# Self-attention on one core: the tile's probabilities are turned before the scores of two tiles ahead, instead of after

## The chip, the cores and the metric

The kernel runs on one NeuronCore of a Trainium2 chip. A NeuronCore has engines with instruction streams of their own, which meet only through semaphores: TensorE (PE in the profile; PEld is its weight loads), VectorE (DVE), ScalarE (ACT), GpSimd (POOL) and SyncE (SP, which issues DMAs). The metric is the time on the device of one execution in microseconds; the median over several runs is quoted.

## What is computed

The kernel is a chain of four transformer parts on an input of 2 x 512 tokens of width 128. Two of them hold a self-attention with 16 heads of width 64; these two are what the change touches. Cut to what matters:

```python
# first part, per batch of 512 tokens, h = adaptive layernorm of x
q, k, v = h @ wq, h @ wk, h @ wv                 # 16 heads of 64
attn = softmax(q @ k.T / sqrt(64))               # 512 x 512 per head
x = (attn @ v) @ wo + bo + x
...
# second part: the same sizes, with biases, a rotary turn of q and k, and a causal mask
q, k = rope(q + q_b), rope(k + k_b)
attn = softmax(where(causal, q @ k.T / sqrt(64), -inf))
```

After them come a cross-attention and a gated feed-forward in the first part, 32 experts in the second, six transformer layers with 8-wide heads in the third and 64 experts in the fourth. None of their code is changed.

## The kernel before

Both self-attentions are one function, `self_attention_block`, called with the name A1 (tiles `A_...` in the profile) and with the name B1 (`B_...`). It works through 16 pairs of heads (8 pairs, two batches). A pair n has four tiles t of 128 queries; step i = 4n + t is one tile of the two heads. In A1 a tile has 512 keys, in B1 it has 128 (t + 1), for the causal mask. Five pieces belong to a tile:

- `scores(i)` (TensorE, L631): two matmuls, one for each head, into two of four PSUM banks, alternating between even and odd tiles; in B1 two small matmuls (L635) add the mask. It waits until the exponentials of tile i - 2 have left its banks, and at t = 0 until q and k of the pair are there.
- `row_max(i)` (VectorE, L817): the negated maximum of each row, of both heads at once.
- `exps(i)` (ScalarE, L729): two exponentials with their row sums, from PSUM to `prob`.
- `weights(i)` (VectorE, L823 and L826): the reciprocal of the sums, and two multiplications of `prob` in place.
- `turn(i)` (TensorE, L647): the 2 x keys/128 transposes of the normalised tile into banks of a ring of three (4, 5, 7); ScalarE's `copy_turned(i)` (L739) empties them into `probT`.

Pair by pair there are also the projections of q, k and v of pair n + 2 (L615, L612), the product with v of pair n - 1 (`weigh`, L661) and the output projection of pair n - 2 (`project_out`, L669). VectorE takes q and k out of PSUM (`take`; L796 and L798 in A1). In B1 ScalarE adds the bias (L717), VectorE multiplies by the cosine (L805), and a DMA and GpSimd do the sine half of the rotary turn (L567, L570).

Each engine's order is written out by hand, as a loop over i, and each engine runs its own list in that order. TensorE's list in a step before the change: `scores(i + 2)`, `turn(i)`, `weigh(n - 1, t)`, one projection of pair n + 2 at t below 3, and `project_out(n - 2)` at t = 3. VectorE's: an output addition (L834) at t = 0, `take` at t = 1 and 2, `row_max(i + 2)`, `weights(i + 1)`, and then small pieces of norms or of the router that were put there to fill. ScalarE's: the copy of a context at t = 0, in B1 a raw copy at t = 1 and 2, `copy_turned(i)`, the copy of v at t = 2, `exps(i + 2)`.

Of the kernel before, what the change touches and what calls it, by code (L numbers as in the profile page):

```python
# [493 lines left out]
def self_attention_block(nc, m, name, w, w_loaded, rope=None, bias=None, tail=None, opening=None):  # L494
# [28 lines left out]
    def turned(i):  # L523

        n, t = divmod(i, TB)
        if 2 * keys(t) <= S:
            return [(("p", i, 0), (0, 1))]
        return [(("p", i, 0), (0,)), (("p", i, 1), (1,))]
# [12 lines left out]
    with nc.sbuf_tensor(name + "_q", [P, 3, S], F32) as qT, \  # L541
# [43 lines left out]
        def _(pe):  # L585
# [4 lines left out]
            def fill(key):  # L590
                bank = RING[len(turns) % len(RING)]
                turns.append(key)
                uses[bank] += 1
                place[key] = bank, uses[bank]
                if uses[bank] > 1:
                    pe.wait_ge(emptied[bank], uses[bank] - 1)
                return bank
# [3 lines left out]
            def project(n, what):  # L601
                if n not in begun:
                    begun.append(n)
                    for (first, _), loaded in zip(W_PARTS, w_loaded):
                        if first == n:
                            pe.wait_ge(loaded, 16)
                    if n == PAIRS and opening is not None:
                        drained(pe, "turn_norm")
                bank = fill((what, n))
                if what == "v":  # L610
                    for t in range(TB):
                        last = pe.matmul(ps[:, bank, t * P:(t + 1) * P], lhsT=hT(n)[:, t * P:(t + 1) * P],  # L612
                                         rhs=weight(n, WV), start=True, stop=True)
                else:
                    last = pe.matmul(ps[:, bank, :], lhsT=weight(n, column[what]), rhs=hT(n), start=True, stop=True)  # L615
                last.then_inc(filled[bank], 1)

            def scores(i):
                n, t = divmod(i, TB)
                if t == 0:  # L620
                    if rope is None:
                        drained(pe, ("q", n))
                        drained(pe, ("k", n))
                    else:
                        pe.wait_ge(q_ready, n + 1)
                        pe.wait_ge(k_ready, n + 1)
                if i >= 2:
                    pe.wait_ge(exp_done, 2 * (i - 1))
                first = S_BANK + 2 * (i % 2)
                for h in range(2):  # L630
                    last = pe.matmul(ps[:, first + h, 0:keys(t)], lhsT=qT[half(h), n % 3, t * P:(t + 1) * P],  # L631
                                     rhs=kT[half(h), n % 3, 0:keys(t)], start=True, stop=not causal)
                if causal:
                    for h in range(2):
                        last = pe.matmul(ps[:, first + h, t * P:(t + 1) * P], lhsT=m.identb[:], rhs=m.maskq[:],  # L635
                                         start=False, stop=True)
                last.then_inc(s_done, 1)

            def turn(i):
                n, t = divmod(i, TB)  # L640
                pe.wait_ge(p_ready, 2 * (i + 1))
                for key, heads in turned(i):
                    bank = fill(key)
                    for j, h in enumerate(heads):
                        for kt in range(keys(t) // P):
                            col = j * keys(t) + kt * P
                            last = pe.transpose(ps[:, bank, col:col + P], prob[:, i % 2, h, kt * P:(kt + 1) * P],  # L647
                                                m.ident[:])
                    last.then_inc(filled[bank], 1)

            def weigh(n, kt):
                if kt == 0:
                    drained(pe, ("v", n))
                    for t in (TB - 2, TB - 1):
                        for key, _ in turned(n * TB + t):
                            drained(pe, key)
                    if n:
                        pe.wait_ge(cT_ready, n)
                q0 = first_q(kt)
                for h in range(2):  # L660
                    last = pe.matmul(ps[half(h), PV_BANK, q0:S], lhsT=v[:, n % 4, kt, half(h)],  # L661
                                     rhs=probT[:, n % 2, kt, h, q0:S], start=kt == 0, stop=kt == TB - 1)
                last.then_inc(pv_done, 1)

            def project_out(n):
                pe.wait_ge(cT_ready, n + 1)
                bank = fill(("out", n))
                for t in range(TB):
                    last = pe.matmul(ps[:, bank, t * P:(t + 1) * P], lhsT=cT[:, n % 2, t * P:(t + 1) * P],  # L669
                                     rhs=weight(n, WO), start=True, stop=True)  # L670
                last.then_inc(filled[bank], 1)
# [9 lines left out]
                project(1, what)  # L681
            for i in range(STEPS):
                n, t = divmod(i, TB)
                if i + 2 < STEPS:
                    scores(i + 2)
                turn(i)
                if n:
                    weigh(n - 1, t)
                if n + 2 < N and t < 3:
                    project(n + 2, "qkv"[t])  # L690
                if t == TB - 1 and n >= 2:
                    project_out(n - 2)
                if opening is not None and (n, t) == (PAIRS - 4, 3):
                    bank = fill("turn_norm")
                    opening.outer[1].turn(pe, ps[:, bank, :]).then_inc(filled[bank], 1)
                if tail is not None:
                    tail.tensor(pe, n, t, ring)
# [2376 lines left out]
```

## Time and profile before

| | |
|---|---|
| time, median of 3 runs | 2410.42 us (2408.8 to 2411.71) |
| the profiled execution | 2412.81 us, of which 2411.0 us are the span of the trace |
| TensorE matmuls | 2076.3 us busy (86%), 10944 instructions |
| VectorE | 1533.4 us (64%) |
| ScalarE | 1267.0 us (53%) |
| GpSimd | 233.7 us (10%) |
| granted TensorE clock, mean | 0.931 of full speed |

The profiled execution lies 2.4 us above the median. The shares are averages over parts with different limits; the two self-attentions lie at about 23 to 290 us and 450 to 682 us of the span. A busy TensorE in this table means that matmuls follow each other, with ends that the profiler models.

### The profile page before, as it was taken

What the parts mean: (1) busy time and instruction counts of PE and PEld (TensorE: products, weight loads), DVE (VectorE), ACT (ScalarE), POOL (GpSimd) and SP (SyncE); (2) the same over time, 40 slices, a digit from 0 to 9 for tenths busy, and PEclk for the clock granted to TensorE, in tenths of its full rate; (3) what the DMA queues carried; (4) which work ended last, traced back from release to release, by engine and by line L of the source; (5) the groups of instructions that cost most, each with busy time, mean ns of one, the idle gap of its engine ahead of it and who ended that gap; (6) DMA issues with size and microseconds to landing.
All of it is one profiled execution on the core that took longest, in us unless ns stands there. A gap on an engine that the chain in (4) does not pass through costs nothing.

```text
span 2411.0 us, 32117 instructions
## 1 busy us (share of the span) xinstructions
PE 2076.3 (86%) x10944; PEld 913.2 (38%) x10944; DVE 1533.4 (64%) x3684; ACT 1267.0 (53%) x2430; POOL 233.7 (10%) x235
## 2 busy tenths in 40 slices
PE   7999998799999888788878887887888788868998
PEld 3444465455566422322233223323222322233433
DVE  6867576666757777467656755774667467553564
ACT  4666553477643356546636563656466556625311
POOL 0000000243320200100010001100010101020000
PEclk9999999799999989979988997999799979979999
DMA  4000000411010110001000100100110001020000
GB/s 157 1 1 1 1 1 1 137 41 40 32 56 3 47 27 1 13 15 46 1 27 1 46 1 27 40 7 1 27 46 1 25 3 28 27 84 1 1 0 9
DMA packets 43154, 61.66 MB, mean 26 GB/s; under 512 B 6097, under 2 KB 35570, under 8 KB 41586
## 3 DMA queue, kind: packets, MB, share of 16 engines
q1 hardware_dynamic: 42994, 59.61, 7.7%
q8 instruction: 90, 1.47, 0.2%
q14 instruction: 70, 0.57, 0.1%
HBM read 31.28 MB, written 0.52 MB: 13 GB/s over the span
## 4 chain that ended last, share of the span: by engine, by line
PE 42%; DVE 10%; ACT 9%; issue 4%; SPq 0%; POOL 0%; ACTq 0%; DMA 0%; DVEq 0%
PE ps L1969 8%; PE ps L1949 5%; ACT big L2457 4%; PE ps L1930 4%; DVE C_nm L2634 4%; PE ps L2014 3%; PE ps L2097 3%; PE ps L2204 2%; PE ps L2200 2%; PE ps L2225 2%; PE ps L2109 2%; ACT big L2537 2%; PE ps L2116 2%; PE ps L2125 2%; PE ps L2074 2%
## 5 line engine op out<-in xcount | busy, mean ns | idle before, releaser
L2634 DVE TENSOR_REDUCE C_nm<-ps 128x1 f32<-128x512 f32 x768 | 500.2, 684 | 214.3 <-PE ps L1930 211.7
L2457 ACT ACTIVATE big<-ps 128x512 f32<-128x512 f32 x768 | 427.7, 596 | 230.6 <-PE ps L1949 220.6
L1930 PE MATMUL ps<-C_attn 62*128 62x512 bf16 x768 | 277.5, 420 | 58.7 <-DVE C_nm L2634 51.1
L1949 PE MATMUL ps<-C_attn 64*128 64x512 bf16 x768 | 253.0, 396 | 64.6 <-ACT big L2457 55.4
L1969 PE MATMUL ps<-big,C_attn 128*32 128x512 f32 x1536 | 214.3, 631 | 14.4 <-ACT big L2457 14.4
L1930 PEld LDWEIGHTS ps<-C_attn 62*128 62x128 bf16 x768 | 63.3, 94 | 296.1 <-DVE C_nm L2634 157.2
L1949 PEld LDWEIGHTS ps<-C_attn 64*128 64x128 bf16 x768 | 59.2, 93 | 279.9 <-ACT big L2457 206.3
L2537 ACT ACTIVATE big<-ps,C_biasx 77x512 f32<-77x512 f32 x192 | 115.5, 678 | 56.4 <-PE ps L2101 56.3
L2390 POOL TENSOR_SCALAR lnv<-mv 128x4 f32<-128x4 f32 x36 | 8.2, 227 | 1218.0 <-DVE mv L2616 1218.0
L2596 ACT ACTIVATE big<-ps 128x512 f32<-128x512 f32 (+1 forms) x66 | 39.4, 597 | 150.0 <-PE ps L2200 149.9
L817 DVE TENSOR_REDUCE A_nm<-ps 128x2 f32<-128x1024 f32 x64 | 78.3, 1224 | 42.6 <-PE ps L631 42.2
L2949 DVE TENSOR_TENSOR big<-big,ps 128x512 f32<-128x512 f32 x64 | 44.0, 687 | 94.5 <-PE ps L2204 74.3
L2724 DVE TENSOR_REDUCE C_nmx<-ps 128x4 f32<-128x308 f32 x192 | 78.0, 471 | 40.5 <-PE ps L2078 40.2
L739 ACT ACTIVATE A_pT<-ps 128x512 f32<-128x512 f32 x128 | 69.6, 598 | 63.6 <-PE ps L647 63.6
L2014 PE MATMUL ps<-C_hT,C_w 128*128 128x512 f32 x144 | 86.1, 705 | 10.7 <-ACT C_hT L2481 5.3
L2841 DVE SCALAR_TENSOR_TENSOR y<-ps,cn,y 128x128 f32<-128x128 f32 x256 | 72.0, 344 | 33.8 <-PE ps L2043 32.8
L729 ACT ACTIVATE A_p<-ps,A_nm 128x512 f32<-128x512 f32 x128 | 87.3, 699 | 9.4 <-DVE A_nm L817 9.4
L2564 ACT ACTIVATE pair<-ps,big 128x512 f32<-128x512 f32 x64 | 43.9, 687 | 78.0 <-PE ps L2036 77.9
L2043 PEld LDWEIGHTS ps<-big,pair 128*128 128x128 f32 x512 | 67.3, 193 | 35.7 <-issue 31.3
L2656 DVE RECIPROCAL C_rden<-ps 128x16 f32<-128x16 f32 x96 | 24.3, 253 | 88.7 <-PE ps L1977 53.3
L729 ACT ACTIVATE B_p<-ps,B_nm 128x128 f32<-128x128 f32 (+3 forms) x128 | 66.3, 526 | 20.9 <-DVE B_nm L817 20.8
L2097 PE MATMUL ps<-C_qx,C_kc 32*77 32x512 f32 x384 | 66.3, 764 | 12.4 <-issue 6.6
(369 smaller groups left out, 3769.1 us busy)
## 6 DMA issues: line engine op xcount, KB each, us to landing
C_attn<-C_first SPq DMA_DIRECT2D x144, 128.0 KB, 2.4
B_rot<-B_rot SPq DMA_DIRECT2D x64, 128.0 KB, 2.0
C_w<-in_C_w SPq DMA_DIRECT2D x6, 1090.0 KB, 5.3
C_attn<-in_D_ew SPq DMA_DIRECT2D x4, 1536.0 KB, 10.2
big<-in_B_ew SPq DMA_DIRECT2D x8, 514.0 KB, 9.1
normw_later<-in_norm_w SPq DMA_DIRECT2D x1, 2304.0 KB, 16.1
A_w<-in_A_w SPq DMA_DIRECT2D x2, 1024.0 KB, 11.2
A_w<-in_A_w SPq DMA_DIRECT2D x2, 768.0 KB, 11.7
```

Of the source, the lines that this page charges most:

```text
L729: act.activation(prob[:, i % 2, h, 0:keys(t)], ps[:, S_BANK + 2 * (i % 2) + h, 0:keys(t)], ACT.Exp, bias=nm[:, i % 2, h:h + 1], accum_out= ...
L817: dve.tensor_reduce(nm[:, i % 2, :], ps[:, first:first + 2, 0:keys(t)], AX.X, ALU.max, negate=True)\
L1930: pe.matmul(ps[:, bank, :], lhsT=qs[side(hp, MAX_ROW), b, 2 * q + pq, t * P:(t + 1) * P], rhs=ks[side(hp, MAX_ROW), b, 2 * q + pq, :], sta ...
L1949: pe.matmul(ps[:, bank, :], lhsT=ks[side(1 - hp, HALF), b, 2 * q + pq, kt * P:(kt + 1) * P], rhs=qs[side(1 - hp, HALF), b, 2 * q + pq, :], ...
L1969: last = pe.matmul(ps[ct * VW:(ct + 1) * VW, PV_BANK, :], lhsT=va[:, b, kt, q * QUAD + ct, :], rhs=prob[:, kt % 2, ct // 2, ct % 2, :], st ...
L2014: pe.matmul(ps[:, bank, :], lhsT=weight(n, col), rhs=hT[:], start=True, stop=True)\
L2097: pe.matmul(ps[0:CTX, banks[r], :], lhsT=cross.k[rows, c, q, :], rhs=qx[rows, :], start=True, stop=False)
L2457: act.activation(prob[:, kt % 2, pq, 1 - hp, :], ps[:, bank, :], ACT.Exp, scale=SCALE)\
L2537: act.activation(probx[:, q % 2, r, :], ps[0:CTX, bank, :], ACT.Exp, bias=cross.bias[:, b:b + 1], scale=SCALE).then_inc(emptied[bank], 1)
L2634: dve.tensor_reduce(nm[:, q % 2, t, pq, hp:hp + 1], ps[:, bank, :], AX.X, ALU.max, negate=True).then_inc(emptied[bank], 1)
L2724: dve.tensor_reduce(nmx[:, t, 4 * r:4 * r + 4], ps[:, bank, 0:4 * CTX].rearrange("p (j k) -> p j k", k=CTX), AX.X, ALU.max, negate=True).t ...
L2841: dve.scalar_tensor_tensor(y, ps[:, bank, t * P:(t + 1) * P], e_b.gates[:, b * TB + t, e:e + 1], y, ALU.mult, ALU.add).then_inc(y_added if ...
```

## The change

Two statements of TensorE's loop change places. In a step TensorE now issues `turn(i)` first and `scores(i + 2)` second; all other engines' lists, the buffers, the waits and the semaphore counts are the same. `scores` uses no bank of the ring, so the banks that the ring hands out are the same too.

```diff
@@ -681,9 +681,9 @@
                 project(1, what)
             for i in range(STEPS):
                 n, t = divmod(i, TB)
+                turn(i)
                 if i + 2 < STEPS:
                     scores(i + 2)
-                turn(i)
                 if n:
                     weigh(n - 1, t)
                 if n + 2 < N and t < 3:
```

## Rows read from the trace of the kernel before

**Rows 1.** Busy time by stretch: inside A1, all of B1, a stretch of B1.

```profile
core 0: us, PE busy (x) PEld busy (x) DVE busy (x) ACT busy (x) POOL busy (x), PEclk, DMA share, GB/s
109.07:258.30 149.23, 149.23 (x758) 71.62 (x756) 106.02 (x206) 96.35 (x235) 0.00 (x0) 1.00 0.00 1
460.00:674.00 214.00, 201.95 (x1214) 107.24 (x1213) 154.35 (x342) 148.53 (x401) 83.00 (x60) 0.98 0.10 38
601.90:612.00 10.10, 8.48 (x53) 5.94 (x54) 8.72 (x23) 5.64 (x17) 4.63 (x4) 0.83 0.08 28
```

**Rows 2.** Timeline, one step of A1: start, duration, engine, line, operation.

```profile
153.79 1.13 PE L631 MATMUL ps<-A_k,A_q 64*128 64x512 f32 x4
...
154.97 1.23 DVE L817 TENSOR_REDUCE A_nm<-ps 128x2 f32<-128x1024 f32 x1 [1.97 <-PE ps L631]
...
156.30 0.88 DVE L826 TENSOR_SCALAR A_p<-A_p,A_inv 128x512 f32<-128x512 f32 x2
...
157.97 1.13 PE L631 MATMUL ps<-A_k,A_q 64*128 64x512 f32 x4
```

**Rows 3.** Timeline, the first steps of A1, TensorE.

```profile
30.80 1.13 PE L631 MATMUL ps<-A_k,A_q 64*128 64x512 f32 x4
...
40.72 1.09 PE L647 MATMUL ps<-ident,A_p 128*128 128x128 f32 x8
...
41.75 1.13 PE L631 MATMUL ps<-A_k,A_q 64*128 64x512 f32 x4
```

**Rows 4.** Timeline, near the end of A1: the multiplications and the turn of tile 62.

```profile
277.38 0.88 DVE L826 TENSOR_SCALAR A_p<-A_p,A_inv 128x512 f32<-128x512 f32 x2
...
278.31 1.09 PE L647 MATMUL ps<-ident,A_p 128*128 128x128 f32 x8 [0.28 <-DVE A_p L826]
```

**Rows 5.** Timeline, one pair of B1, four steps.

```profile
541.59 0.92 PE L631 MATMUL ps<-B_k,B_q 64*128 64x384 f32 x4
...
542.76 0.96 DVE L817 TENSOR_REDUCE B_nm<-ps 128x2 f32<-128x768 f32 x1 [0.38 <-PE ps L635]
...
544.94 1.13 PE L631 MATMUL ps<-B_k,B_q 64*128 64x512 f32 x4
...
546.42 1.22 DVE L817 TENSOR_REDUCE B_nm<-ps 128x2 f32<-128x1024 f32 x1
...
547.75 0.75 DVE L826 TENSOR_SCALAR B_p<-B_p,B_inv 128x384 f32<-128x384 f32 x2
...
548.51 0.49 PE L631 MATMUL ps<-B_k,B_q 64*128 64x128 f32 x4
...
549.77 0.69 DVE L805 TENSOR_TENSOR B_k<-B_rot,B_cos 128x512 f32<-128x512 f32 x1 [1.28 <-ACTq L720]
...
550.38 0.42 DVE L817 TENSOR_REDUCE B_nm<-ps 128x2 f32<-128x256 f32 x1
...
550.91 1.36 DVE L826 TENSOR_SCALAR B_p<-B_p,B_inv 128x512 f32<-128x512 f32 x2
...
551.48 0.70 PE L631 MATMUL ps<-B_k,B_q 64*128 64x256 f32 x4
...
552.44 0.69 DVE L817 TENSOR_REDUCE B_nm<-ps 128x2 f32<-128x512 f32 x1 [0.17 <-PE ps L635]
...
553.24 0.68 DVE L826 TENSOR_SCALAR B_p<-B_p,B_inv 128x128 f32<-128x128 f32 x2
...
554.81 0.92 PE L631 MATMUL ps<-B_k,B_q 64*128 64x384 f32 x4
```

**Rows 6.** Timeline, VectorE and GpSimd in a later pair of B1.

```profile
602.70 1.27 POOL L570 TENSOR_TENSOR B_q<-B_q,B_rot 128x512 f32<-128x512 f32 x1
...
602.71 1.81 DVE L805 TENSOR_TENSOR B_k<-B_rot,B_cos 128x512 f32<-128x512 f32 x1
```

**Rows 7.** Timeline, TensorE: turn of the first tile of B1's pair 1.

```profile
476.81 0.39 PE L647 MATMUL ps<-ident,B_p 128*128 128x128 f32 x2
```

**Rows 8.** Timeline, TensorE: turns of B1's tiles 56 and 62.

```profile
655.26 0.39 PE L647 MATMUL ps<-ident,B_p 128*128 128x128 f32 x2
...
670.98 0.87 PE L647 MATMUL ps<-ident,B_p 128*128 128x128 f32 x6 [0.39 <-DVE B_p L826]
```

## The prediction

> **What bounds the kernel now.** I read the page first, then the busy time by stretch, then the timelines of single steps. The page says that TensorE is busy most of the span, but what counts is the two self-attentions. By stretch, TensorE is busy for all of 149.23 us of 149.23 inside A1, and for 201.95 of 214.00 us in B1, at a granted clock of 1.00 and 0.98 [rows 1]. So both are bound by TensorE's own work; VectorE is busy 71% and 72% there. The reader should see in the timeline that in A1 one step follows the next after 4.18 us (scores at 153.79 and at 157.97) with four pieces of TensorE work in it, and that VectorE, after its row maximum, has to wait 1.97 us for the next scores [rows 2]. In B1 a pair takes 13.22 us, from the scores at 541.59 to those at 554.81, by the same rule [rows 5]. A change of TensorE's order adds and removes no work. It can gain only idle TensorE time, of which A1 has none and B1 12 us, and it loses if it makes a chain through the other engines longer than TensorE's own work.
>
> **The chain that the change closes.** No instruction is added; what moves is the eight or fewer transposes of turn(i), with their weight loads, past the scores of tile i + 2. No DMA moves. The new wait is in the order: scores(i + 2) now stands behind turn(i), which waits for weights(i). Now look at VectorE, whose list is row_max(i + 2), then weights(i + 1). The row maximum waits for scores(i + 2); weights(i + 1), whose exponentials were ready long before, is queued behind it; and turn(i + 1) on TensorE waits for weights(i + 1). So turn(i), scores(i + 2), row_max(i + 2), weights(i + 1), turn(i + 1) become one chain, and a step cannot be shorter than that. Before, the scores came ahead of the turn, and the chain from one turn to a later one spread over two steps: the multiplications ended at 157.18 (156.30 + 0.88) [rows 2], some 1.9 us ahead of the turn that needs them, which follows the scores of 157.97.
>
> **A1, one step.** Turn to scores, when the one follows the other directly: 40.72 to 41.75, 1.03 us [rows 3]. Start of scores to start of the row maximum: 153.79 to 154.97, 1.18 us; start of the row maximum to the end of the multiplications: 154.97 to 157.18, 2.21 us [rows 2]. End of the multiplications to the turn that waits for them: 278.26 to 278.31, 0.05 us [rows 4]. Sum: 4.47 us, against TensorE's 4.18 us in a full step and about three quarters of that in the steps of the first and last pairs that have only three pieces. The chain wins in all of them. What VectorE does besides (taking q or k, 512 columns like the 0.69 us product of [rows 5], and small pieces of norms) falls into the 2.26 us in which it now waits for turn and scores; ScalarE's copies fall into its idle time, 53 us of 149 [rows 1]. I cost both at nothing; without that cover each would add its excess over 2.26 us, once.
>
> The first turn can start at 30.80, where the scores of tile 2 stand now [rows 3]; 62 steps of 4.47 us bring the turn of tile 62 to 307.9, where it is at 278.31 now [rows 4]: +29.6 us. Two steps carry four more transposes of a norm (4 x 0.13 us), so TensorE's 4.7 us sets them: +0.4. A1: **+30 us**. Bounds: 4.42 us a step if the 0.05 us is already in the rows, 4.57 if TensorE restarts 0.1 us later after a wait: +27 to +36.
>
> **B1, one pair.** The four steps differ, because tile t has 128 (t + 1) keys. Scores to row maximum is 1.17 us for 384 keys and 0.96 us for 256 [rows 5]; by the difference I take 1.38 for 512 and 0.75 for 128. A transpose is 0.13 us. From the turn at t = 0 as zero:
> - t = 0: the chain (two transposes, 384 keys) is shorter than TensorE's work, 541.59 to 544.94 [rows 5]. Turn of t = 1 at 3.35.
> - t = 1: 0.52 for four transposes and 1.38 bring the row maximum of 512 keys to 5.25. The multiplications would end 2.08 us later (546.42 to 548.50 [rows 5]): turn of t = 2 at 7.38.
> - t = 2: the row maximum of 128 keys stands behind VectorE's cosine product, which waits for a raw copy on ScalarE, which is queued behind the exponentials of the 512 keys. That path from row maximum to row maximum is 546.42 to 550.38, 3.96 us [rows 5]; so 9.21, later than the scores allow. The multiplications end 1.89 us on (550.38 to 552.27): turn of t = 3 at 11.15.
> - t = 3: 1.03 for eight transposes, 0.96, then 552.44 to 553.92 [rows 5], 1.48, and 0.05: next pair at 14.67.
>
> That is 14.67 us against 13.22. VectorE and GpSimd also get in each other's way here. A cosine product that took 0.69 us [rows 5] took 1.81 us where a GpSimd addition had started 0.01 us before it [rows 6], so a new phase can cost up to 1.12 us a pair: 15.8 at most. If on the contrary the raw copy held nothing up and the multiplications of 512 keys took A1's 0.88 us [rows 2] and not 1.36 [rows 5], it would be 13.9. I take 14.9, a fifth of the way up, because the delayed product leaves the multiplications behind it undelayed.
>
> The Trainium skill, "SBUF — State Buffer", section "SBUF: two separate sides", says that VectorE's products of two SBUF operands and GpSimd share a port pair as an exclusive lock, and that the one that comes second is blocked for the other's whole instruction. Rows 6 agree: 1.81 us where the other took 1.27. By that rule alone, with GpSimd first in every pair, the pair would be 15.8 us and the total 12 us above mine.
>
> Pairs 1 to 13 take 178.45 us now, from 476.81 [rows 7] to 655.26 [rows 8], 6.6 us over 13 x 13.22, through the router's pieces. Half of that should hide in VectorE's new waits (an estimate): 13 x 14.9 + 3.3 = 197.0, +18.6. The last six steps with scores take 15.72 us now (655.26 to 670.98 [rows 8]); without projections and GpSimd the chain gives about 3.1, 4.0, 3.0, 3.5, 3.1 and 4.0, 20.7, +5.0. Pair 0 has no product with v and gains up to 3 us of chain: +1.5. B1: **+25 us**. Bounds +7 (13.9 us a pair, all pieces hidden, nothing for pair 0) and +42 (15.8, nothing hidden, 3 us for pair 0).
>
> **Sum.** +30 and +25 are +55 us. The profiled execution, 2412.8 us with 1.8 us around its span, would become 2468; on the median of 2410.4 that is **2466 us**. Nothing after either block starts early enough to take it back: both end in a barrier.
>
> **Rivals.**
> 1. The clock falls. In 601.90 to 612.00 TensorE was idle 1.62 us, and the granted clock was 0.83, between the levels of 1.2 and 2.4 GHz [rows 1]: 10.10 x 0.17, 1.7 us of work lost. The change makes idle gaps of 1 to 1.5 us in each pair of B1 and in some nine steps of A1. A fall in each of these 22 places is +37 us: 2503. Against it: 0.3 us of idleness in a 4.47 us step leaves A1 94% busy, the share that B1 has now at 0.98.
> The skill's "TensorE: Matmul & The Clock Gate", Part 1, says that the throttled clock is the default and sustained activity releases it; rows 1 agree in the direction, and by it this rival only adds to the loss.
> 2. Only A1 pays, because B1's pairs stay near 13.9 us and its pieces hide: +30 and a few, about 2443.
> 3. TensorE stays the bound and nothing changes: 2410. That needs a chain under 4.18 us, 0.29 us less than the rows give, as if VectorE took weights(i + 1) before row_max(i + 2). Its list says otherwise.
> 4. It gets faster: with that same chain hidden, a turn that is ready would no longer wait behind scores that wait for q and k out of the rotary turn, as in B1's first pair. It decides only from a chain under 4.18 us on, and its ceiling is B1's idle 12 us [rows 1]: 2398.
>
> **Chances and range.** The forecast holds 0.76, the falling clock 0.10, A1 alone 0.06, no change 0.04, faster 0.04. The bounds of both blocks give +34 to +78, 2444 to 2488; rivals 2 and the mild form of 1 lie at its ends. About 0.2%, 5 us, is what a measurement here can tell from no change: slower 0.92, within it 0.04, faster 0.04.
>
> **What would show it.** In A1, scores 4.47 us apart in every step, with TensorE idle about 0.3 us before the turn, released by VectorE's L826, and some 1.4 us in the steps without projection; the first multiplications' end followed by a turn within 0.1 us. VectorE's row maximum waits for L631, and weights follows at once. A1 ends 30 us later at a clock of 1.00. In B1 pairs of 14.7 to 15.2 us, with the longest step at t = 2. After both, everything at its old length. The prediction is wrong if turns do not wait for L826, if A1's steps stay at 4.18, or if the clock falls below 0.95 in either block.

## The result, and the profile after

| | before | after |
|---|---|---|
| time, median | 2409.61 us (2406.32 to 2411.71, 4 runs) | 2489.8 us (2484.65 to 2496.45, 4 runs) |
| span of the profiled execution | 2411.0 us | 2490.6 us |
| TensorE matmuls busy | 2076.3 us | 2093.2 us |
| mean granted clock | 0.931 | 0.929 |

The ratio is 1.0336, with an interval of 1.0306 to 1.0365: 80 us slower. The forecast was 2466 us, with 2444 to 2488 as its range, so the time came out 24 us above the forecast and 2 us above the range. The 79.6 us by which the span grew lie like this, read from the first and last turns of the two blocks: A1 ends 29.0 us later (its last turn starts at 309.38 instead of 280.35), the stretch between the blocks gives back 1.0, B1 is 52.2 us longer, and the rest gives back 0.6. A1 did what was forecast; B1 did twice as much.

**A1.** The timeline of one step of the kernel after, which answers to [rows 2]. Columns: start, duration, engine, line, operation, and in brackets the idle time before it and what ended it.

```profile
150.61 1.09 PE L647 MATMUL ps<-ident,A_p 128*128 128x128 f32 x8 [0.22 <-DVE A_p L826]
...
151.63 1.13 PE L631 MATMUL ps<-A_k,A_q 64*128 64x512 f32 x4
...
152.81 1.22 DVE L817 TENSOR_REDUCE A_nm<-ps 128x2 f32<-128x1024 f32 x1 [2.25 <-PE ps L631]
...
154.14 0.88 DVE L826 TENSOR_SCALAR A_p<-A_p,A_inv 128x512 f32<-128x512 f32 x2
...
155.08 1.09 PE L647 MATMUL ps<-ident,A_p 128*128 128x128 f32 x8 [0.22 <-DVE A_p L826]
```

The reader should walk the chain link by link: turn at 150.61, scores 1.02 us later, the row maximum 1.18 after those, the end of the multiplications at 155.02, and the next turn 0.06 after that, 4.47 us in all. Each row either waits for the one above it or stands behind it in its engine's list. The waits from 29 to 290 us, grouped by who waited for whom (us in total, times, longest), say the same for most steps; in the kernel before, the second of these rows read 0.5 us for two waits.

```profile
DVE A_nm L817 <- PE ps L631: 85.1, 58, 2.3
...
PE ps L647 <- DVE A_p L826: 22.0, 56, 2.3
```

**B1.** Busy time by stretch, kernel after: B1's pair 0, pairs 1 to 13 and pairs 14 and 15, and at last all of A1 (columns as in [rows 1]: length, busy time of PE, PEld, DVE, ACT and POOL, PEclk, DMA share).

```profile
488.74:510.54 21.80, 14.56 (x58) 8.27 (x56) 13.53 (x20) 9.80 (x26) 10.66 (x8) 0.68 0.13 48
510.54:729.91 219.37, 188.64 (x1045) 99.50 (x1045) 138.37 (x274) 125.36 (x339) 69.22 (x52) 0.94 0.09 32
729.91:753.59 23.68, 17.98 (x111) 8.55 (x109) 15.55 (x48) 13.53 (x39) 0.00 (x0) 1.00 0.00 1
29.51:309.38 279.87, 253.68 (x1269) 119.47 (x1269) 180.85 (x378) 170.13 (x404) 0.00 (x0) 1.00 0.00 1
```

The same three stretches of the kernel before:

```profile
460.76:476.81 16.05, 10.70 (x59) 6.07 (x57) 14.74 (x19) 8.32 (x23) 10.77 (x8) 0.89 0.18 66
476.81:655.26 178.45, 173.81 (x1046) 92.40 (x1045) 124.16 (x275) 127.21 (x344) 72.23 (x52) 0.99 0.11 39
655.26:673.40 18.14, 16.08 (x104) 7.95 (x103) 14.77 (x47) 12.35 (x36) 0.00 (x0) 1.00 0.01 2
```

Pair 0 pays 5.75 us (forecast 1.5), pairs 1 to 13 pay 40.9 (forecast 18.6), the last two 5.5 (forecast 5.0 for their six steps). VectorE's busy time in the middle row is 14.2 us longer although its instructions are the same: something stretches them. One pair of B1 shows what, in the timeline of the kernel after, which answers to [rows 5, 6]:

```profile
535.82 0.87 PE L647 MATMUL ps<-ident,B_p 128*128 128x128 f32 x6 [0.32 <-DVE B_p L826]
...
536.97 1.27 POOL L570 TENSOR_TENSOR B_q<-B_q,B_rot 128x512 f32<-128x512 f32 x1
...
537.04 1.75 DVE L805 TENSOR_TENSOR B_k<-B_rot,B_cos 128x512 f32<-128x512 f32 x1 [1.28 <-ACTq L720]
...
538.71 0.41 DVE L817 TENSOR_REDUCE B_nm<-ps 128x2 f32<-128x256 f32 x1
...
540.17 1.09 PE L647 MATMUL ps<-ident,B_p 128*128 128x128 f32 x8 [1.17 <-DVE B_p L826]
...
542.95 1.49 DVE L826 TENSOR_SCALAR B_p<-B_p,B_inv 128x128 f32<-128x128 f32 x2
543.03 1.32 POOL L570 TENSOR_TENSOR B_k<-B_k,B_rot 128x512 f32<-128x512 f32 x1
...
544.49 0.44 PE L647 MATMUL ps<-ident,B_p 128*128 128x128 f32 x2 [0.93 <-DVE B_p L826]
```

GpSimd's addition for q starts 0.07 us ahead of VectorE's cosine product for k, and the product takes 1.75 us instead of 0.69; then GpSimd's addition for k starts 0.08 us behind the multiplications of the next tile, and these take 1.49 instead of 0.48, which is their time one pair earlier (at 527.83). The 0.68 of [rows 5] is not their undisturbed time: there too a GpSimd product was running, from 552.38 to 553.65. Both stand in the closed chain, and TensorE's turn waits for both. Grouped by line, the cosine product of k reads so before, and then after (count, busy time, mean ns):

```profile
L805 DVE TENSOR_TENSOR B_k<-B_rot,B_cos 128x512 f32<-128x512 f32 x16 | 14.2, 889 | 15.5 <-ACTq L720 15.3
```

```profile
L805 DVE TENSOR_TENSOR B_k<-B_rot,B_cos 128x512 f32<-128x512 f32 x16 | 23.4, 1462 | 14.4 <-ACTq L720 14.2
```

Of its 16 instances 12 took 1.4 us or more, against 3 before. The Trainium skill, "SBUF — State Buffer", section "SBUF: two separate sides", describes VectorE and GpSimd excluding each other on a shared pair of ports; the trace agrees, with 1.75 us for 0.69.

**The clock in B1.** The timeline of TensorE in pair 0 of the kernel after, and below it the busy time of pair 1, pairs 2 to 8 and pairs 9 to 13 (columns as above):

```profile
493.25 1.12 PE L647 MATMUL ps<-ident,B_p 128*128 128x128 f32 x4 [2.15 <-DVE B_p L826]
494.30 2.08 PE L631 MATMUL ps<-B_k,B_q 64*128 64x512 f32 x4
...
500.25 1.54 PE L647 MATMUL ps<-ident,B_p 128*128 128x128 f32 x6 [2.66 <-DVE B_p L826]
```

```profile
510.54:528.36 17.82, 15.44 (x72) 6.99 (x72) 9.45 (x18) 9.09 (x26) 5.13 (x4) 0.82 0.08 31
528.36:639.41 111.05, 95.69 (x561) 50.17 (x561) 69.84 (x133) 68.17 (x185) 37.57 (x28) 1.00 0.09 34
639.41:729.91 90.50, 77.51 (x413) 42.35 (x413) 59.09 (x124) 48.10 (x129) 26.53 (x20) 0.89 0.08 30
```

After 2.15 us of idleness the scores of 512 keys, 1.13 us elsewhere, take 2.08; the granted clock reads 0.50 from 493.2 to 496.4, the lower of TensorE's two levels, 1.2 GHz. The granted clock is 0.68 over pair 0 and 0.94 over pairs 1 to 13, against 0.89 and 0.99 before. Pairs 2 to 8 run at 1.00 and are slow all the same, 15.86 us each. In A1 the clock stays at 1.00.

### The profile page after: what moved, and what is told of

It is laid out like the page before. It is cut to its first block, busy times and chain, and to the rows that moved or that the text cites. A ratio compares the mean times of both kernels' runs of the same rounds, so it can differ in the third digit from the quotient of the medians.

```text
span 2490.6 us, 32117 instructions
## 1 busy us (share of the span) xinstructions
PE 2093.2 (84%) x10944; PEld 921.9 (37%) x10944; DVE 1543.8 (62%) x3684; ACT 1271.5 (51%) x2430; POOL 230.8 (9%) x235
## 4 chain that ended last, share of the span: by engine, by line
PE 39%; DVE 10%; ACT 8%; issue 4%; SPq 1%; DMA 0%; POOL 0%; ACTq 0%; DVEq 0%
PE ps L1969 7%; PE ps L1949 5%; ACT big L2457 4%; PE ps L1930 4%; DVE C_nm L2634 4%; PE ps L2097 3%; PE ps L2014 2%; PE ps L2204 2%; PE ps L2200 2%; PE ps L2225 2%; ACT big L2537 2%; PE ps L2109 2%; PE ps L2116 2%; PE ps L2125 2%; PE ps L2074 1%
## 5 line engine op out<-in xcount | busy, mean ns | idle before, releaser
L817 DVE TENSOR_REDUCE B_nm<-ps 128x2 f32<-128x256 f32 (+1 forms) x64 | 52.6, 822 | 68.9 <-PE ps L635 68.5
L647 PE MATMUL ps<-ident,A_p 128*128 128x128 f32 x512 | 70.2, 280 | 26.8 <-DVE A_p L826 26.2
L647 PE MATMUL ps<-ident,B_p 128*128 128x128 f32 x320 | 52.5, 299 | 40.6 <-DVE B_p L826 39.1
## 6 DMA issues: line engine op xcount, KB each, us to landing
normw_later<-in_norm_w SPq DMA_DIRECT2D x1, 2304.0 KB, 15.8
```

The source lines that it names most:

```text
L817: dve.tensor_reduce(nm[:, i % 2, :], ps[:, first:first + 2, 0:keys(t)], AX.X, ALU.max, negate=True)\
```

## The experiments

The theory was that turn, scores, row maximum and multiplications form one chain, closed by VectorE's list; that the chain alone sets A1; and that in B1 collisions with GpSimd stretch it. The rival was that the turn's place itself, or the clock, costs the time. The ratios below are to the kernel before, run beside each.

**Opening the chain.** The changed kernel, with VectorE's list turned round in both blocks:

```diff
+                if i + 1 < STEPS:
+                    weights(i + 1)
                 if i + 2 < STEPS:
                     row_max(i + 2)
-                if i + 1 < STEPS:
-                    weights(i + 1)
```

> The changed kernel with VectorE's list turned as well: weights(i + 1) ahead of row_max(i + 2). Theory (the chain is closed by VectorE's order): turn(i + 1) no longer waits for scores(i + 2), the chain is spread over two steps again and TensorE's own work sets the step. A1: steps of 4.15 to 4.18 us, B1: pairs of 13.2 to 13.8 us, time within 12 us of the kernel before, 2398 to 2422. Rival (it is turn(i)'s own wait for weights(i) that holds the scores up, whatever VectorE's order is): A1 stays at 4.47 us a step and the time above 2465.

2439.41 us (2433.78 to 2440.79), ratio 1.0093 (1.0066 to 1.0119): 23 us over the kernel before. That lies between the two expectations: A1's steps came out shorter than the theory's 4.15 to 4.18 us, B1's pairs longer than its 13.2 to 13.8. By block, A1 takes 254.8 us from first to last turn (changed kernel 279.9, before 248.5) and B1 236.4 (264.9 and 212.6). The timeline of A1 in this kernel:

```profile
145.09 1.08 PE L661 MATMUL ps<-A_pT,A_v 128*64 128x512 f32 x4 [0.38 <-ACT A_cT L748]
...
151.06 1.04 PE L647 MATMUL ps<-ident,A_p 128*128 128x128 f32 x8
...
152.16 0.88 DVE L826 TENSOR_SCALAR A_p<-A_p,A_inv 128x512 f32<-128x512 f32 x2
...
155.09 1.04 PE L647 MATMUL ps<-ident,A_p 128*128 128x128 f32 x8
```

The multiplications end at 153.04, 2.05 us before the turn that needs them, and the step from 151.06 to 155.09 is 4.03 us: the chain is open, and in these steps the new place of the turn costs nothing by itself. What is left in A1 is one step in four, at t = 0, of 4.44 to 4.51 us in most pairs, where the product with v now waits for ScalarE's copy of the context (first row), and the three-piece steps. In B1's pairs 2 to 8 a pair takes 14.5 to 15.3 us, and the step at t = 2 still 4.28 to 4.97.

**What still holds B1.** The same kernel, with VectorE's `take` moved behind the multiplications too, so that its list is `weights(i + 1)`, `take`, `row_max(i + 2)`:

```diff
+                if i + 1 < STEPS:
+                    weights(i + 1)
                 if n + 2 < N and t in (1, 2):
                     take(n + 2, t - 1)
                 if i + 2 < STEPS:
                     row_max(i + 2)
-                if i + 1 < STEPS:
-                    weights(i + 1)
```

> Theory: in B1 what still held the turn after VectorE took the multiplications ahead of the row maximum was the cosine product that stood ahead of both and waits for ScalarE's raw copy. With the product behind the multiplications the longest step of a pair (t = 2, 4.35 to 4.97 us) falls to about 3.7, a pair of B1 from 14.8 to 13.3 to 13.7 us, B1 from 236 to 215 to 222, and the total lies 5 to 16 us above the kernel before (A1's 6 us stay). Rival: the product stands in front of the row maximum in any case, so the wait only moves there, a pair stays over 14.3 us and the total 20 us or more above.

2437.87 us (2433.23 to 2442.12), ratio 1.011 (1.0088 to 1.0132). In B1 the theory held in the main: the step at t = 2 is 3.24 us in most of pairs 2 to 8, a pair there about 13.8 (13.3 to 13.7 expected), and the block 224.15 us (215 to 222 expected), 12 less than in the experiment above. The total missed the theory's 5 to 16 us and stayed 25 above the kernel before, where the rival had it, though not by the rival's pairs of over 14.3 us. A1 took back half of the gain, 6 us; the other half is no more than the intervals of the two runs leave open. A1's first and last turn now lie 260.7 us apart, with steps of 4.22 to 4.36 us at t = 2, where the projection of v waits for the later `take` of k:

```profile
158.58 0.97 PEld L612 LDWEIGHTS ps<-A_w,hT 128*128 128x128 f32 x8 [1.01 <-DVE A_k L798]
```

In B1 of the same timeline a collision stretches the multiplications to 1.90 us and costs the turn only 0.30, since they start early:

```profile
533.74 1.90 DVE L826 TENSOR_SCALAR B_p<-B_p,B_inv 128x512 f32<-128x512 f32 x2
...
533.85 1.50 POOL L570 TENSOR_TENSOR B_q<-B_q,B_rot 128x512 f32<-128x512 f32 x1
...
535.69 0.86 PEld L647 LDWEIGHTS ps<-ident,B_p 128*128 128x128 f32 x8 [0.30 <-DVE B_p L826]
```

**One block at a time.** The new order under `if rope is None` (A1 alone) and under `if rope is not None` (B1 alone), as an edit of the kernel before:

```diff
+                if rope is None:          # the other kernel: is not None
+                    turn(i)
                 if i + 2 < STEPS:
                     scores(i + 2)
-                turn(i)
+                if rope is not None:      # the other kernel: is None
+                    turn(i)
```

> The new order in A1 alone, B1 in the old order. Theory (62 steps of 4.47 us, nothing given back): +29 us, 2439. Rival (the profiled spans of A1 overstate it, part is hidden at the barrier or in later loads): +20 or less. B1's first turn to last turn stays at 213 us in both.

> The new order in B1 alone, A1 in the old order. Theory (both blocks add, B1's loss is of its own making): +51 us, 2461, with the same three lengths of step as in the changed kernel, 3.4, 4.05 and 4.35 or 5.43 us. Rival (B1's extra loss comes from a phase or a clock that A1's longer run left behind): +25 to +35, 2435 to 2445.

A1 alone: 2448.47 us, ratio 1.0131 (1.0097 to 1.0165), +32. B1 alone: 2467.83, ratio 1.0215 (1.0189 to 1.0241), +52. Together 84, against 80 for the whole change, which is equal within the intervals: the blocks don't touch each other, and the shares read from the trace (29 and 52) are right.

**GpSimd taken out of the way.** In the changed kernel and in the kernel before, GpSimd's product and addition (L567, L570) work on 8 of 512 columns, so most of the sine half of the rotary turn is left out; all waits stay.

```diff
-    pool.tensor_tensor(turned_rows, turned_rows, rope[i][1], ALU.mult).then_inc(sin_done, 1)
+    pool.tensor_tensor(turned_rows[:, 0:8], turned_rows[:, 0:8], rope[i][1][:, 0:8], ALU.mult)\
+        .then_inc(sin_done, 1)
...
-    pool.tensor_tensor(dst[:, n % 3, :], dst[:, n % 3, :], turned_rows, ALU.add)\
+    pool.tensor_tensor(dst[:, n % 3, 0:8], dst[:, n % 3, 0:8], turned_rows[:, 0:8], ALU.add)\
```

> The changed kernel with GpSimd's sine product and addition cut to 8 of 512 columns, so that most of the rotary turn's sine half is left out; all waits and the order stay. Theory (what my sum missed in B1 is VectorE's multiplications and cosine products blocked behind GpSimd's): pairs 2 to 8 fall from 15.9 to about 14.2 us (the chain's 14.67 less the 0.48 us that the multiplications of 512 keys lose), t = 2 and t = 3 have one length each, and the time falls by 20 to 35 us to 2455 to 2470. Rival 1 (the raw copy on ScalarE and the order alone): pairs stay at 15.4 to 15.9 and the time above 2480. Rival 2 (the clock): the pairs at a lower clock, 0, 1 and 9 to 13, keep their length.

> The kernel before with the same cut as the run before it (GpSimd's sine product and addition on 8 of 512 columns, most of the sine half left out). Theory (GpSimd blocks VectorE off TensorE's path in the old order, except in the first pair and the router's pairs): pairs 2 to 8 stay at 13.2 us, only the first pair and pairs 10 to 13 gain; 6 to 14 us faster, 2402 to 2410. Rival (GpSimd's work costs the old order as much as the new, so the cut says nothing of the change): 40 us or more faster.

Changed kernel with the cut: 2447.78 us, ratio 1.0145 (1.011 to 1.0179). Against the changed kernel's 1.0336 that is 1.9% of the kernel before, some 46 us, and more than expected. Kernel before with the cut: 2396.53, ratio 0.9928 (0.9902 to 0.9954), 17 us faster, a little more than the 6 to 14 expected. Busy time by stretch, the same three stretches of B1, first the changed kernel with the cut, then the kernel before with it:

```profile
487.81:502.19 14.38, 9.61 (x57) 5.16 (x57) 8.91 (x20) 9.72 (x26) 1.72 (x8) 1.00 0.20 75
502.19:689.26 187.07, 178.78 (x1045) 94.90 (x1045) 111.35 (x274) 123.24 (x339) 12.73 (x52) 0.99 0.10 37
689.26:712.94 23.68, 17.98 (x110) 8.55 (x109) 15.56 (x48) 13.53 (x39) 0.00 (x0) 1.00 0.01 1
```

```profile
452.67:465.13 12.46, 10.66 (x58) 6.60 (x57) 8.17 (x20) 8.46 (x23) 1.73 (x8) 0.86 0.23 85
465.13:637.52 172.39, 170.49 (x1047) 90.72 (x1045) 110.77 (x275) 126.98 (x344) 10.70 (x52) 1.00 0.11 41
637.52:655.67 18.15, 16.08 (x104) 7.95 (x103) 14.78 (x47) 12.36 (x36) 0.00 (x0) 1.00 0.01 2
```

Without GpSimd's work the change costs B1 1.9 + 14.7 + 5.5 = 22.1 us, and with it 52.2. So 30 of B1's 52 us come from VectorE and GpSimd meeting. Less work on GpSimd also makes q and k ready earlier, but that is not where the time goes: from 488 to 754 us of the changed kernel no wait of TensorE, VectorE or ScalarE is put down to GpSimd. The clock came back in the same run, from 0.68 and 0.94 to 1.00 and 0.99; the two gaps of pair 0 are then 1.30 and 1.26 us instead of 2.15 and 2.66, so in the changed kernel the falls go with the waits that the collisions made. (The kernel before stays at 0.86 in its pair 0 even so.) In pairs 2 to 8 the changed kernel's clock is 1.00 with GpSimd's work and without it, and a pair takes 15.86 and 14.07 us: 12.6 us over these seven pairs are stretched instructions alone, against 0.9 in the same pairs of the kernel before. How the rest divides between the stretched instructions and the lower clock behind them was not measured.

**A known delay put into the chain.** A memset of 128 x 512 on VectorE between `row_max` and `weights`, in A1 alone, in the kernel before and in the changed kernel:

```diff
                 if i + 2 < STEPS:
                     row_max(i + 2)
+                if rope is None:
+                    c.after(dve.memset(pad[:], 0.0))
                 if i + 1 < STEPS:
                     weights(i + 1)
```

> The kernel before with a memory set of 128 x 512 put into VectorE's list between row_max(i + 2) and weights(i + 1), in A1 alone; it costs VectorE an estimated 0.5 us a step. Theory (the multiplications end some 1.9 us before the turn needs them): hidden in every full step, 4.15 to 4.18 us a step as before; 0 to +4 us from the steps with three pieces. Rival (VectorE's time counts in the old order too): +25 to +35 us.

> The changed kernel with the same memory set at the same place, in A1 alone. Theory (row_max and weights lie on the closed chain, so every addition between them counts in full): A1's steps grow from 4.47 us by the whole cost of the memory set, about 5.0 us, and the time by 62 times that, +25 to +37 us over the changed kernel, 2515 to 2527. Rival (TensorE's pieces or ScalarE's set the 4.47 us): under +8.

Before: 2412.26 us, ratio 0.9997 (0.9977 to 1.0017); nearly all full steps stay at 4.15 to 4.18 us, and A1 is 2.7 us longer, as expected. Changed: 2546.81, ratio 1.0551 (1.0522 to 1.0579), 2.15% or 52 us over the changed kernel, of which 46 lie in A1 (325.6 us from first to last turn). That is more than expected, since the size was off: the delay with the wait for its completion is 0.66 us, not the memset's 0.48. The timeline of the changed kernel with the memset (lines below it are moved by one):

```profile
150.18 1.09 PE L648 MATMUL ps<-ident,A_p 128*128 128x128 f32 x8 [0.89 <-DVE A_p L827]
...
152.45 1.23 DVE L818 TENSOR_REDUCE A_nm<-ps 128x2 f32<-128x1024 f32 x1 [1.26 <-PE ps L632]
...
153.73 0.48 DVE L856 MEMSET A_pad<- 128x512 f32 x1
154.25 0.17 DVE L824 RECIPROCAL A_inv<-A_sums 128x2 f32<-128x2 f32 x1
...
155.38 1.09 PE L648 MATMUL ps<-ident,A_p 128*128 128x128 f32 x8 [0.95 <-DVE A_p L827]
```

From the row maximum's start to the reciprocal it is 1.80 us instead of 1.14, and nearly all full steps take 5.14 instead of 4.47: the delay comes out whole. The kernel before hides the same delay whole. That is the difference between a chain that sets the step and one with slack.

**The order that pays.** From the kernel before, in A1's pairs 1 to 13 alone: the turn first and the multiplications first; and, in all of A1, ScalarE's copy of the context moved from t = 0 to t = 3 of the pair before, ahead of the exponentials. Everything else keeps its order.

```diff
+                if rope is None and 1 <= n <= N - 3:
+                    turn(i)
                 if i + 2 < STEPS:
                     scores(i + 2)
-                turn(i)
+                if not (rope is None and 1 <= n <= N - 3):
+                    turn(i)
...
+                early = rope is None and 1 <= n <= N - 3
+                if early:
+                    weights(i + 1)
                 if i + 2 < STEPS:
                     row_max(i + 2)
-                if i + 1 < STEPS:
+                if i + 1 < STEPS and not early:
                     weights(i + 1)
...
-                if t == 0 and n >= 2:
+                if t == 0 and n >= 2 and rope is not None:
                     copy_context(n - 2)
...
+                if rope is None and t == 3 and 1 <= n < N - 1:
+                    copy_context(n - 1)
```

> The new order with VectorE's weights(i + 1) first, in the full steps of A1 alone (pairs 1 to 13), and the copy of the context on ScalarE moved from the head of a pair to the step before, ahead of its exponentials; B1 and A1's other pairs in the old order. Theory (with the chain open, TensorE's pieces follow each other in 4.00 to 4.03 us where the old order took 4.15 to 4.18, and the first step of a pair loses 0.45 us only to that copy): pairs of 16.1 us instead of 16.65, 5 to 8 us faster than the kernel before, ratio 0.997. Rival (the shorter steps are paid back at the borders of the pairs): within 0.2% of before.

2405.87 us (2398.05 to 2416.0, 12 runs) against 2413.4 for the kernel before on that chip; ratio 0.9976 (0.9957 to 0.9996). It is 0.24% faster than the kernel before, an interval that only just excludes no change, and the fastest of those tried that leave nothing out. The timeline of TensorE:

```profile
163.49 1.04 PE L647 MATMUL ps<-ident,A_p 128*128 128x128 f32 x8
...
164.45 1.13 PE L631 MATMUL ps<-A_k,A_q 64*128 64x512 f32 x4
...
165.51 1.08 PE L661 MATMUL ps<-A_pT,A_v 128*64 128x512 f32 x4
...
166.52 1.16 PE L612 MATMUL ps<-A_w,hT 128*128 128x128 f32 x8
167.52 1.04 PE L647 MATMUL ps<-ident,A_p 128*128 128x128 f32 x8
```

No row waits, and the step is 4.03 us. The block takes 242.9 us instead of 248.5.

**The same for B1.** The last kernel, with B1's pairs 1 to 13 in the new order too, and there VectorE's list `weights`, `take`, `row_max`.

> The faster version of A1, and in B1's pairs 1 to 13 the turn first with VectorE's list multiplications, cosine product, row maximum. By the theory a pair of B1 takes 13.0 to 13.7 us against 13.1 to 13.3 before, so the total is within 8 us of the version that changes A1 alone, on either side. By the rival a pair stays over 14.3 us and the total is 12 us or more above the kernel before.

2414.95 us, ratio 1.0014 (1.0001 to 1.0027), 9 us over the version that changes A1 alone and so a little outside the 8 us expected; the two were run on different chips. B1's pairs 2 to 8 take 13.6 to 14.7 us, 13.9 on average, just above the theory's 13.0 to 13.7, and the block 222.6 us against 212.6. The chain is open in B1 as well, but collisions still reach the turn (steps of 3.9 to 4.2 us where 3.2 is usual), and the new order gains nothing there.

## Why the prediction was right in A1 and short in B1

- **TensorE bounds both blocks, and a change of order can only lose or gain idle time.** Right: the instructions are the same and no new kind of work appeared.
- **The chain.** Right, and shown from both sides: the turn waits for L826 in 56 steps of A1; taking the multiplications ahead of the row maximum brings the step from 4.47 to 4.03 us; a delay of 0.66 us in the chain lengthens the step by 0.67.
- **A1: 4.47 us a step, +30 us.** Measured 4.45 to 4.47 us in 51 of the 62 steps (4.52 to 4.62 in the others), and the block ends 29.0 us later, at a clock of 1.00.
- **B1, the steps at t = 0 and t = 1.** 3.40 and 4.05 us against 3.35 and 4.03. Right.
- **B1, the steps at t = 2 and t = 3.** This is the step that failed: "a new phase can cost up to 1.12 us a pair: 15.8 at most". I allowed one collision a pair, priced it at a fifth, and called its full price the bound. The price of one collision was right (1.75 against 0.69 us is 1.06), but it came in 12 of 16 pairs, and in five of pairs 2 to 8 a second one came, at t = 2 or at t = 3. A pair took 15.86 us on average in pairs 2 to 8 (528.36 to 639.41) and 18.1 in pairs 9 to 13 (639.41 to 729.91). The wrong thought behind it was "the delayed product leaves the multiplications behind it undelayed": GpSimd does one product and one addition for q and one of each for k, and in a chain without slack each of the four can meet something. A second collision, from the timeline of the kernel after:

```profile
570.50 1.97 DVE L826 TENSOR_SCALAR B_p<-B_p,B_inv 128x512 f32<-128x512 f32 x2
570.92 1.26 POOL L567 TENSOR_TENSOR B_rot<-B_rot,B_sin 128x512 f32<-128x512 f32 x1 [1.42 <-DMA B_rot<-B_rot]
...
572.52 1.09 PE L647 MATMUL ps<-ident,B_p 128*128 128x128 f32 x8 [2.26 <-DVE B_p L826]
```

- **B1, the bare chain.** With GpSimd out of the way in both kernels the three terms of +18.6, +1.5 and +5.0 measured +14.7, +1.9 and +5.5, 22 against 25. That these sums lie so close is in part luck. The forecast's chain of 14.67 us a pair already held collisions: the 1.36 us for the multiplications of 512 keys and the 0.68 for those of 128, taken from [rows 5], are 0.88 and 0.48 without GpSimd's work, and a pair of the bare chain took 14.07. On the other side, pairs 1 to 13 of the kernel before become 6 us shorter without it (178.45 to 172.39), which the forecast did not take off. What was mis-sized is the collision term. The forecast put 0.23 us a pair on its chain, so 14.9 is 0.83 above the measured bare chain; pairs 2 to 8 of the changed kernel lie 1.79 above it. Over both kernels GpSimd's part of the loss is 2.0 us a pair (40.9 - 14.7 = 26.2 us over pairs 1 to 13), and 5.75 - 1.9 = 3.9 for pair 0; a part of both, in pairs 0, 1 and 9 to 13, is the clock.
- **Rival 1, the falling clock.** It came in part. Not in A1, as the argument against it said. In B1 the mean was 0.92, under the 0.95 that the prediction named as its own refutation, with pair 0 at 0.68. I had taken gaps of 1 to 1.5 us; with the collisions two of pair 0 became 2.15 and 2.66.
- **Rivals 2 to 4.** B1 paid in full, and nothing stayed or became faster. Rival 4's condition, a chain under 4.18 us, was made by hand in the version that pays; the gain there did not come from B1's idle time, as rival 4 had it, but from A1's own steps.
- **After each block**, everything kept its length, within 1.0 us.

## What to carry to other kernels

Before two statements of one engine's list change places, write the chain through the other engines' lists from the moved piece back to itself; if it closes within one step, its length, not the busiest engine's work, is the new step, and every delay on it counts in full. When slack goes, price every transfer or neighbour that can touch the chain at its full stretched duration and once for each time it runs, not once a pair. The repair belongs to the other engine's list: take first what is ready, then what waits for the moved piece.

## What the runs showed of the hardware that was not expected

- **The same four pieces take TensorE a different time in a different order.** Scores, turn, product with v, projection: 4.15 to 4.18 us a step [rows 2], with TensorE busy throughout [rows 1]. Turn, scores, product, projection: 4.00 to 4.03 us with no wait, from 163.49 to 167.52 in the version that pays. From turn to scores it is 0.96 us, from scores to product 1.06, from product to projection 1.01, from projection to turn 1.00. Why was not tried. In B1 the same order brought no gain.
- **A stretch's busy share does not tell its clock.** Kernel before, the stretch from 601.90 to 612.00 us: TensorE busy 8.48 of 10.10 us, at 0.83 [rows 1]. Kernel after, pairs 14 and 15: busy 17.98 of 23.68 us, a smaller share, at 1.00. Pair 0 of B1 there: 14.56 of 21.80 at 0.68, with gaps of 2.15 and 2.66 us. The Trainium skill's "TensorE: Matmul & The Clock Gate", Part 1, has the clock rise with sustained activity; A1, busy without a long gap at 1.00, and pair 0 agree in direction.
